# A transformer block on one core: ScalarE's order inside a feed-forward tile, and who does the last additions

## The reference, cut to what matters

```python
x = x + attn(cond(x, cond_128, ...), Wq, Wk, Wv, Wo, ...)      # 32 heads of 128, 8 key/value heads
f = cond2(x, cond_128, ...)                                    # each sequence mixed by its own 32x32 matrix
gate_proj = (gate_w - gate_z) * gate_s      # 512 x 1792, one zero and scale per 128 rows and column
up_proj   = (up_w - up_z) * up_s
down_proj = (down_w - down_z) * down_s      # 1792 x 512
x = x + (silu(f @ gate_proj) * (f @ up_proj)) @ down_proj
```

## Time and profile before

| | us |
|---|---|
| median of 3 runs (lowest, highest) | 691.26 (690.58, 691.94) |
| the profiled execution | 690.25 |
| its span on the core | 688.5 |
| busy in it: TensorE, VectorE, ScalarE, GpSimd | 665.3, 559.3, 417.1, 450.4 |
| start of the first gate product, start of tile 2, end of tile 26 | 504.69, 524.48, 670.89 |

### The profile page before, as it was taken

One profiled execution on the slowest core, in us unless ns is written; L12 is line 12 of the kernel. 1 busy time (PEld: TensorE's weight loads), 2 busy tenths in 40 slices (PEclk: granted clock), 3 DMA queues, 4 the chain that ended last, 5 costly groups with the idle time before them and its releaser, 6 DMA issues.

```text
span 688.5 us, 14465 instructions
## 1 busy us (share of the span) xinstructions
PE 665.3 (97%) x5004; PEld 375.2 (54%) x5004; DVE 559.3 (81%) x845; ACT 417.1 (61%) x1257; POOL 450.4 (65%) x377
## 2 busy tenths in 40 slices
PE   9999999999999999999999999999989999999995
PEld 8766555656656565565656656566544434444341
DVE  4967878969878887986977889677776998898887
ACT  0478572844647475474655738447465778877773
POOL 0468874873776496387558548737537678887885
PEclk9999999999999999999999999999999999999999
DMA  7420354575386267437426735442200356555554
GB/s 255 182 93 1 124 149 99 126 211 81 92 146 195 77 153 206 100 65 234 100 91 151 200 78 126 125 87 79 48 1 1 58 97 115 106 124 123 96 97 106
DMA packets 98799, 79.15 MB, mean 115 GB/s; under 512 B 79520, under 2 KB 80064, under 8 KB 96576
## 3 DMA queue, kind: packets, MB, share of 16 engines
q1 hardware_dynamic: 94864, 65.97, 37.2%
q0 software_dynamic: 3456, 12.58, 9.8%
q10 hardware_dynamic: 432, 0.01, 0.0%
HBM read 48.01 MB, written 2.21 MB: 73 GB/s over the span
## 4 chain that ended last, share of the span: by engine, by line
PE 62%; DVE 12%; POOL 11%; issue 9%; ACT 3%; DMA 1%; SPq 1%; DVEq 0%; ACTq 0%; POOLq 0%
PE bank L649 17%; PE bank L651 17%; PE bank L650 17%; DVE exact L1934 5%; POOL whole L2185 3%; POOL wqlo L2056 2%; ACT exact L1396 2%; DMA xT<-in_xt 1%; PE bank L839 1%; DVE mx L1522 1%; DVE oTlo L1710 1%; PE bank L1006 1%; PE bank L1007 1%; DVE acc L1954 1%; POOL qn L2092 1%
## 5 line engine op out<-in xcount | busy, mean ns | idle before, releaser
L649 PE MATMUL bank<-wohi,oThi 128*128 128x512 f16 x256 | 97.1, 379 | 3.0 <-DVE oTlo L1710 2.9
L649 PE MATMUL bank<-wqhi,cThi 128*128 128x512 f16 x256 | 97.0, 379 | 0.9 <-POOL wqlo L2056 0.6
L651 PE MATMUL bank<-wohi,oTlo 128*128 128x512 f16 x256 | 97.0, 379 | 0.0
L650 PE MATMUL bank<-wolo,oThi 128*128 128x512 f16 x256 | 97.0, 379 | 0.0
L651 PE MATMUL bank<-wqhi,cTlo 128*128 128x512 f16 x256 | 97.0, 379 | 0.0
L650 PE MATMUL bank<-wqlo,cThi 128*128 128x512 f16 x256 | 97.0, 379 | 0.0
L1162 ACT ACTIVATE qraw<-bank 128x512 f32<-128x512 f32 x64 | 37.8, 590 | 81.5 <-PE bank L651 80.9
L2104 POOL TENSOR_TENSOR qinv<-qms,neghalf 128x8 f32<-128x8 f32 x28 | 56.4, 2014 | 39.6 <-ACT qms L1181 39.6
L2066 POOL TENSOR_TENSOR wolo<-wor,wohi 128x512 f16<-128x512 f32 x32 | 39.7, 1261 | 56.5 <-ACT wohi L1142 56.5
L1173 ACT ACTIVATE qsq<-qraw 128x128 f32<-128x128 f32 x256 | 75.4, 299 | 1.7
L1934 DVE SCALAR_TENSOR_TENSOR exact<-bank,uscl,exact 128x512 f32<-128x512 f32 x84 | 62.8, 747 | 16.6 <-ACT exact L1396 12.8
(11 more groups left out here) (223 smaller groups left out, 1791.4 us busy)
## 6 DMA issues: line engine op xcount, KB each, us to landing
acc<-dprod POOLq DMA_DIRECT2D x24, 512.0 KB, 4.6
wqr<-in_wq SPq DMA_DIRECT2D x8, 1024.0 KB, 7.6
wor<-in_wo SPq DMA_DIRECT2D x8, 1024.0 KB, 6.1
raw<-in_gu_w SPq DMA_DIRECT2D x28, 256.0 KB, 3.1
zeros<-in_gu_z SPq DMA_DIRECT2D x28, 256.0 KB, 4.4
...
```

What stands on the lines that cost most here:

```text
L649: mm(o, ahi, bhi, start=start and k == 0, stop=False)
L650: mm(o, ahi, blo, start=False, stop=False)
L651: last = mm(o, alo, bhi, start=False, stop=stop and k == n - 1)
```

## The change

The diff, cut to its core:

```diff
-            return 2 * n + max(n - DIRECT, 0) + (1, 0, 2, 3)[c]
+            return 2 * n + (0, 0, 1, 1)[max(n - DIRECT + 1, 0)] + (1, 0, 2, 3)[c]
...
-            return 2 * n + (c + 1) // 2 if n < DIRECT else DIRECT + n + 1
+            return 2 * n + (c + 1) // 2 - (n > DIRECT)
...
                 if c == 1:
-                    sp.wait_ge(p_acc, TILES - DIRECT)
+                    sp.wait_ge(p_acc, TILES - DIRECT + 1)
                 else:
...
                     pe.wait_ge(p_wo, G * kv + G)
-                if t == 0:
+                if t == 0 and isinstance(u, int) and u == UNITS - 1:
+                    pe.wait_ge(d_oTlo, BQ * u + 3)
+                    pe.wait_ge(p_oTlo, 1)
+                elif t == 0:
                     pe.wait_ge(d_oTlo, BQ * u + BQ)
...
-            def outputs_high(u):
+            def outputs_whole(b):
+                A(owhole[:, 0:HT], PC[b][:, :], ACT.Copy, scale=O_DOWN).then_inc(a_owhole, 1)
+
+            def outputs_high(u, samples=range(BQ)):
                 act.wait_ge(t_pv, u + 1)
-                for b in range(BQ):
+                for b in samples:
                     A(oThi[:, :, :, b, :], PC[b][:, :].rearrange("p (t g s) -> p t g s", t=HQ, g=G), ACT.Copy,
...
                 act.wait_ge(t_dn, down_done(n, c))
-                if n == DIRECT + 2:
+                if n == TILES - 1:
                     act.wait_ge(p_acc, 1)
...
             turned_high(3)
+            outputs_high(UNITS - 1, (3,))
+            outputs_whole(3)
             scaled(0, 0)
             scaled(0, 2)
-            outputs_high(UNITS - 1)
+            outputs_high(UNITS - 1, (0, 1, 2))
             up_first(0)
...
                 scaled(n, 2)
-                hidden_high(n - 1)
-                up_first(n)
                 if n >= LAG:
                     down_scaled(n - LAG, 1)
+                up_first(n)
+                hidden_high(n - 1)
                 if n in (2, 3):
...
                 gate(n)
+            down_scaled(TILES - 2, 1)
             hidden_high(TILES - 1)
-            down_scaled(TILES - 2, 1)
+            down_scaled(TILES - 2, 3)
             down_scaled(TILES - 1, 1)
...
-            def outputs_low(u):
-                for b in range(BQ):
-                    dve.wait_ge(a_oThi, BQ * u + b + 1)
+            def outputs_low(u, samples=range(BQ)):
+                for b in samples:
+                    dve.wait_ge(a_oThi, BQ * u + b + 1 + (u == UNITS - 1))
                     V.scalar_tensor_tensor(oTlo[:, :, :, b, :], PC[b][:, :].rearrange("p (t g s) -> p t g s", t=HQ, g=G),
...
                         dve.wait_ge(l_acc, down_moved(n))
+                    elif c == 3:
+                        dve.wait_ge(p_acc, 3)
                     elif i:
...
             scaled(0, 1)
+            scaled(0, 3)
+            outputs_low(UNITS - 1, range(3))
             hidden_power(0)
-            scaled(0, 3)
-            outputs_low(UNITS - 1)
             up_added(0)
...
                     last_hidden()
+            down_added_to(DIRECT, 3)
             hidden_low(TILES - 1)
-            down_added_to(DIRECT, 3)
-            for c in (0, 2, 3):
+            for c in (0, 2):
                 down_added_to(TILES - 2, c)
...
-            def add_down(n):
-                pool.wait_ge(a_dn, down_evicted(n, 1))
-                if n == DIRECT:
+            def add_down(n, c, before):
+                pool.wait_ge(a_dn, down_evicted(n, c))
+                if before:
+                    pool.wait_ge(p_acc, before)
+                else:
                     pool.wait_ge(l_acc, down_moved(n))
-                else:
-                    pool.wait_ge(p_acc, n - DIRECT)
-                o = acc[:, 1, place(1), :]
-                Q.tensor_tensor(o, o, dprod[:, n % 2, 0, :], ALU.add).then_inc(p_acc, 1)
+                if c == 3:
+                    pool.wait_ge(d_dn, down_added(n - 1, c))
+                o = acc[:, 1, place(c), :]
+                Q.tensor_tensor(o, o, dprod[:, n % 2, c // 2, :], ALU.add).then_inc(p_acc, 1)
...
                 hidden_product(0)
+                outputs_low(3)
                 feature_scale(0)
...
                                 ALU.mult).then_inc(p_fscl, 1)
+
+            def outputs_low(b):
+                pool.wait_ge(a_owhole, 1)
+                Q.tensor_tensor(oTlo[:, :, :, b, :], owhole[:, 0:HT].rearrange("p (t g s) -> p t g s", t=HQ, g=G),
+                                oThi[:, :, :, b, :], ALU.subtract).then_inc(p_oTlo, 1)
...
                     feature_scale(1)
+            add_down(DIRECT, 1, 0)
             pool.wait_ge(d_hlo, 1)
-            for n in range(DIRECT, TILES):
-                add_down(n)
+            add_down(TILES - 2, 1, 1)
+            add_down(TILES - 2, 3, 2)
+            add_down(TILES - 1, 1, 3)
```

4 lines of the change are left out of this document (3 added, 1 removed).

## The result

| | us |
|---|---|
| before, beside it on the same chip, median of 7 runs (lowest, highest) | 691.17 (690.58, 692.37) |
| changed kernel, median of 7 runs (lowest, highest) | 687.84 (686.33, 689.0) |
| ratio, 95% interval | 0.9948 (0.9935 to 0.9962) |
| the profiled execution of the changed kernel | 686.33 |

A forecast was written before the change was run, and what follows sets the result against it. TensorE, busy 97%, was taken to lose 6.9 us in tiles 8 to 26 to a loop through ScalarE's order. Terms -5.4 + 0.4 + 0.1 = -4.9 gave a median of 686.4 us, range 683.8 to 690.1.

The forecast's parts named there:

- The ring of ScalarE's order: Once-per-tile loop through VectorE, GpSimd and ScalarE, the up part waiting behind `hT`: 5.61 us a tile, cut by reordering.
- Part 1: ScalarE's tile order, down block 1 and up part ahead of `hT`: -5.4 us, bounds -6.9 and -0.9.
- The floor of 101.9: Time of tiles 8 to 26 at TensorE's own pace with 8 transposition groups, against 108.88 us before.
- The loss that stays: Friction left in tiles 8 to 26 after the reorder: 0.05 us a tile taken, 1.0 us in all.
- three rings: Next bounds per tile: TensorE 5.18 us, a two-tile loop through the SiLU 5.18, one through the DMA 5.05 to 5.5.
- My DMA ring: Two-tile loop: ScalarE's `down_scaled` block 1 waits for the DMA of two tiles earlier; 5.6 us plus the landing, per two tiles.
- Rival 1: The DMA loop binds in every tile: 689.2 us at landings of 5.2 (chance 0.15), 691.1 at 5.4 (0.12 together with rival 4).
- Rivals 2 to 4: No friction, 684.3 us (0.1); longer landings, 695.5 (0.07); order without effect, 691.8 (0.12 together with rival 1 at 5.4).
- rival 3: Slower: the up part hangs on the DMA and landings grow; 695.5 us at a landing of 6.0, chance 0.07.
- Part 2: Last unit's low parts at the start: projection at 510.5, fourth `gate(1)` part at 514.92 for the late hidden scale; costs 0.4 us.
- Part 3: The end, with GpSimd's first `add_down` early and five instead of seven additions on VectorE: +0.1 us.
- the hold: At the end, GpSimd's early addition delays VectorE's low half to 7.7 us after `hidden`: +0.1, against -0.45 without it.

The follow-up runs named there:

- order_only: Kernel before with only ScalarE's new order in the tile (down block 1, up part 0, then the high half): 687.09 us, ratio 0.9946.
- start_back: Changed kernel with the start as before (four low parts on VectorE, hidden scale between the gate's parts): 687.36 us, ratio 0.9943.
- after_no_turn: Changed kernel without the 16 DMAs transposing the second half's input, tiles 14 to 27 fed the first half's: 684.96 us, ratio 0.9905.
- three_late: Changed kernel with three dprod buffers and GpSimd's accumulating DMA issued behind add_part and hidden_low: 695.0 us, ratio 1.0036.
- hup_early: Changed kernel with only the hidden scale moved back ahead of the gate's part 1 on VectorE: 688.37 us, ratio 0.9957.
- ht_first: Changed kernel with ScalarE's last high half ahead of down block 1 of tile 26: 687.96 us, ratio 0.9953.

## Why the prediction was right, and where not

**The mechanism and the sign: right.** The ring of ScalarE's order is cut. Plain tiles run at 5.18 to 5.26, the up part starts behind the scaled block, `hT` last, and no TensorE matmul waits for L1422. order_only shows that this alone is the change. Total: -4.9 forecast, -3.3 measured. But both signs that were to show it wrong came too: tiles of 5.4 and more with ScalarE waiting for the DMA at `dprod` (6 waits, 4.5 us), and a tail shorter by 0.4 or more (0.56 from the start of tile 27). The sign and the main term were right, two terms were not.

**Part 1: mis-sized, -5.4 forecast, -2.8 measured** in this execution, and -2.0 in those of order_only and start_back (106.93 and 106.84 in [8-26]). The bound of -0.9 in the prediction is added up wrongly: -6.9 + 19 x 0.3 + 0.5 is -0.7.

The floor of 101.9 stands. Left over are 106.08 - 101.9 = 4.2 instead of 1.5. The step that failed is "The loss that stays is between 0 and 0.10 a tile", and with it the list of three rings. There is a fourth, over one tile: landing + 0.55, through GpSimd's own wait for the previous DMA. My DMA ring halved the landing over two tiles ((5.6 + L)/2, so 5.5 at L = 5.4); the fourth takes it whole (5.95), and it turns from harmless to binding at a landing of 4.63, just over the ordinary one. The wait stood in the code of `move_down`, but no row of before named a landing as what that DMA waited for, so I didn't price it; that three issues of before came 0.55 after a landing would have told it. Where it binds, `add_part`, on which the SiLU waits, and the low half are queued behind it on GpSimd.

Over half of the 4.2 lies in four tiles: 14, 15, 21 and 26, with landings of 5.35, 5.52, 5.09 and 5.21, took 2.65 more than 4 x 5.18. after_no_turn gives the shares: 1.9 of the 4.2 go with the transposing DMAs, 0.6 is tile 26's landing of 5.21, and 1.7 are left over. That this is about the 1.5 of the forecast is luck: it is no friction spread over all tiles, but 0.36 each in tiles 8 and 17, 0.8 in tiles 15 and 21 with landings of 5.0 and 5.1, and 0.17 in tiles 20 and 24.

**Rival 1: half right.** The bound was a DMA, at landings of 5.0 to 5.5, but in six or so tiles instead of everywhere, and harder in each. The Trainium skill, "SBUF — State Buffer", section "Who interferes with whom", was cited for landings that stay at 4.5 and a time of 685.4. What stretches them in tiles 8 to 14 is other DMAs, on which that rule says nothing; after_no_turn, without those, ran at 684.96. For those of 5.09 in tile 21 and 5.21 in tile 26 the trace shows only the instruction packets beside them.

**Rivals 2 to 4 did not come.** Against rival 3, the landings did not grow with the shorter tile (4.5 to 4.6 in most late tiles). The late issue of three_late shows that side of it: 8.3 us of waits of GpSimd for landings from 560 to 673 us, and a slower kernel.

**Part 2: right, to the tenth.** +0.4 forecast, +0.38 measured, with both of its times within 0.1 us, and hup_early shows the late hidden scale to be the cause.

**Part 3: the hold right, the path and the sum wrong.** +0.1 forecast. Counted as there, from the last `hidden` to the end, before took 688.5 - 672.91 = 15.59 and after 684.5 - 669.35 = 15.15: **-0.4**. The low half came as forecast (7.79 for 7.7), but in the changed kernel by another wait: `down_scaled(26, 1)` waits for the last landing and holds ScalarE's last `hT` by about 0.5, so the low half starts only as GpSimd's addition ends (676.45 and 676.53) and shows 0.69 instead of the stretched 1.2. ht_first, without that wait, shows the hold itself, 7.74 and 1.14. So that the two waits cost the same is luck. The step that failed is "The output's DMAs follow GpSimd's last addition and end where they did". By the earlier trace rows VectorE's seven additions ended at 680.48 + 4.69 = 685.17, 0.45 after GpSimd's 684.72, so VectorE was last. I had both numbers and compared neither.

What won the 0.4 is not part 3, though: order_only still has all seven additions on VectorE, and its end is as short (15.1 from `hidden`). With part 1's shorter tile its low half comes 0.44 sooner, and VectorE, the last to end, with it: 11.83 after `hidden` instead of 12.26. Part 3 then makes the low half 0.58 later and the additions behind it 0.46 shorter (11.95), and is worth nothing that these profiles show.

The terms as measured, -2.80 + 0.38 - 0.44, and -0.22 for the rest (0.10 in tiles 2 to 7, 0.12 from the start of tile 27 to `hidden`), give -3.08 in this pair of executions, against -3.3 between the medians. By order_only the -0.44 is part 1's too.

**Open.** Why a single landing of 6.7 to 6.9 appears in some executions, and how often (each has an instruction packet 4.7 to 5.1 after its issue, but so have some landings of 5.1 to 5.4); whether the ring over one tile could be opened. The wait between two accumulating DMAs cannot simply go: the Trainium skill, "DMA: Bandwidth & Descriptors", section "Rules for kernel authors", says that an accumulating DMA reads its destination and writes it later, so another write to the same bytes in between is lost. No run here shows it, and a kernel with fewer or split accumulating DMAs was not tried.
